# A decoder layer with routed experts: last scatters ahead of a weight split, last destinations ahead of shared rows, and the first four expert tiles waiting for their own expert's splits

## The chip, the cores and the metric

The kernel runs on 1 core of a Trainium2 chip. The metric is device time in microseconds (us), the median of three runs. A core has five engines with a queue each: TensorE (PE), VectorE (DVE), ScalarE (ACT), GpSimd (POOL) and SyncE (SP, which here issues DMA transfers and waits). They meet only in semaphores.

## The reference

The input x is 4 batches of 256 rows of 256 values. One layer adds three sublayers to it, each behind a layer norm without weights:

```
x = x + attn(_layernorm(x))                 # gated memory: sigmoid gates, decaying scan, output product
x = x + xattn(_layernorm(x), ctx)           # softmax over normalised similarities
x = x + ffn(_layernorm(x))

logits = x @ router_w                       # 8 experts
expert_idx = argmax(logits); score = sigmoid(max(logits)); xs = x * score
for e in range(8):
    h = silu(xs @ gate_w[e]) * (xs @ up_w[e])
    out = out + where(expert_idx == e, h @ down_w[e], 0)
shared = silu(x @ shared_gate_w) * (x @ shared_up_w) @ shared_down_w
return out + shared
```

Each of the 1024 rows goes to one expert. All matrices are 256 x 256, but for the router's and the context's.

## The kernel before

**Two stages.** In the first, the four batches pass through steps with names like turn1, similarity, router. Each engine executes its steps in an order written out by hand (PE_ORDER, ACT_ORDER, DVE_ORDER, POOL_ORDER, lines 50 to 76); "name:b" is that step for batch b, and semaphores order the engines among one another. In the second, rows are worked on sorted by expert, in NS = 15 tiles of 128 rows.

**Between them** each batch of 256 rows is routed. TensorE's `rank` counts with matmuls how many rows ahead of each go to the same expert; for the last batch it also counts the rows of each expert. VectorE's `destination` (line 809) makes each row's place from it, and for batch 3 first the counts (`counts_made`). GpSimd's `scatter` (line 456) waits for the destinations and for the metadata (`row_meta`) and writes two tiles of 128 rows with one indirect DMA each to `x_sorted` in HBM. Places without a row get padding: four transfers of SyncE (line 352) and four of ScalarE (line 643, ahead of shared_tanh:3), both behind the counts. VectorE's `slot_table` (line 823) computes for each of the 15 tiles its expert (`te`) and its first row (`tr`); `table_made` says that it is done.

**Shared expert.** For each batch: TensorE's `shared_gu`; ScalarE's `shared_tanh`; VectorE's `shared_hidden`, four products that end in `h_made`; TensorE's `shared_turn`, which waits for them; ScalarE's copy `shared_turned`; TensorE's `shared_down`; and VectorE's `shared_add`, which ends in `base_made`. shared_down:2 also waits for shared_add:1.

**Weights in two parts.** Matrices are multiplied as high and low parts. 21 units of 128 x 512 are loaded (SyncE), rounded (`weight_hi`, ScalarE) and split (`weight_lo`): units 0 to 2 by VectorE, 3 to 20 by GpSimd, line 466, each counting `unit_lo` up by one. Units 3 and 4 are the shared expert's; 5 + 2e and 6 + 2e are expert e's. So unit_lo is 18 when all are there, and 4 + 2e when those of expert e are.

**The expert stage.** SyncE waits for the table, the padding, the scatters and the first four tiles of base_made, and loads four tiles of rows (line 362). TensorE waits for table_made, loads the 15 experts of `te` into registers of its own sequencer (line 1140), waits for all 18 splits (line 1141) and for the down weights, and then runs, per tile: `rows_turn` (transpose), `gate_up`, `hidden_turn`, `down`; ScalarE and VectorE work in between (`rows_hi`, `rows_lo`, `tile_tanh`, `hidden`, `hidden_copy`, `result`). GpSimd adds each tile's result to the output with an indirect DMA (line 480).

Of the kernel before, what the change touches and what calls it, by code (L numbers as in the profile page):

```python
# [24 lines left out]
I32 = mybir.dt.int32  # L25
# [36 lines left out]
    memory:3 turned3_lo:0 residual3:1 sim_stats:2 residual2:3 route:0 sim_scale:2 destination:0  # L62
    turned3_lo:1 residual3:2 sim_stats:3 route:1 shared_hidden:0 sim_scale:3 destination:1
    turned3_lo:2 residual3:3 route:2 shared_hidden:1 destination:2 turned3_lo:3 shared_add:0 route:3
    shared_hidden:2 destination:3 slot_table:3 shared_add:1 shared_hidden:3 shared_add:2
    shared_add:3
""".split()

# [2 lines left out]
    centre:0 sim_rstd:0 weight_lo:7 sim_eps:1 centre:1 weight_lo:8 weight_lo:9 sim_rstd:1 centre:2  # L71
    weight_lo:10 weight_lo:11 weight_lo:12 sim_eps:2 rstd3:0 sim_rstd:2 weight_lo:13 row_meta:0
    sim_eps:3 scatter:0 sim_rstd:3 centre:3 rstd3:1 weight_lo:14 row_meta:1 scatter:1 rstd3:2
    row_meta:2 scatter:2 rstd3:3 row_meta:3 weight_lo:15 scatter:3 weight_lo:16 weight_lo:17
    weight_lo:18 weight_lo:19 weight_lo:20
""".split()

# [7 lines left out]
def decoder_kernel(nc, x, ctx_in, Wv, Wg, bg, Wq, bq, Wo, W_k, b_k, gamma, beta,  # L85
# [3 lines left out]
    E = router_w.shape[1]  # L89
# [16 lines left out]
    ROUNDS = (NS - 3 - PEEL) // TILE_RING  # L106
    RING = 6
    PROJ = 3

    x_sorted = nc.dram_tensor("x_sorted", (E * REGION + P, W), F32, kind="Internal").ap()  # L110
    out_rows = out.rearrange("b s d -> (b s) d")

    with ExitStack() as ctx:
        def sb(name, shape, dt=F32):
            return ctx.enter_context(nc.sbuf_tensor(name, shape, dt))
# [4 lines left out]
        def sem(name):  # L120
            return ctx.enter_context(nc.semaphore(name))
# [11 lines left out]
        xT3_lo = sb("xT3_lo", [P, 2, KT, S], F32R)  # L133
        gqv_hi = sb("gqv_hi", [P, PROJ, KT, D], F32R)
        gqv_lo = sb("gqv_lo", [P, PROJ, KT, D], F32R)
        wo = sb("wo", [P, KT, D])
# [64 lines left out]
        preceding = sb("preceding", [1, NS])  # L201
        tr_f = sb("tr_f", [1, NS])
        te = sb("te", [1, NS], I32)
        tr = sb("tr", [1, NS], I32)
        cnt = sb("cnt", [1, E], I32)
        tid = sb("tid", [P, NS], U32)
# [19 lines left out]
        def ps_row(n):  # L226
            nonlocal spare
            spare += n
            return bT[0:1, spare - n:spare]

        ntile, tile_s, te_f, offset = ps_row(E), ps_row(NS), ps_row(NS), ps_row(NS)
# [7 lines left out]
        unit_hi, proj_lo, unit_lo = sem("unit_hi"), sem("proj_lo"), sem("unit_lo")  # L239
# [32 lines left out]
        def rows(w):  # L272
            return w.rearrange("(k p) n -> p k n", p=P)

        units = [(rows(w), gqv_hi[:, i], gqv_lo[:, i]) for i, w in enumerate((Wg, Wq, Wv))]
# [4 lines left out]
        SHARED_LO = 2  # L280
# [10 lines left out]
        def pad_regions(queue, engine, first, last):  # L291
            _, count = nc.values_load_multi_w_load_instructions(
                cnt[0:1, first:last], engines=[engine], min_val=0, max_val=N,
                skip_runtime_bounds_check_because="a count of tokens is at most all of them")
            for e in range(first, last):
                queue.dma_start(x_sorted[bass.ds(count[e - first] + e * REGION, P), :], pad[:, :]).then_inc(padded, 16)
# [5 lines left out]
        def _(sp):  # L302
# [3 lines left out]
            def load_unit(n):  # L306
                if n >= RING:
                    old = n - RING
                    sp.wait_ge(unit_hi, old + 1)
                    if old < PROJ:  # L310
                        sp.wait_ge(proj_lo, old + 1)
                    else:
                        sp.wait_ge(unit_lo, old - PROJ + 1)
                sp.dma_start(stage[:, n % RING], units[n][0]).then_inc(stage_in[n % RING], 16)

            def load(name, dst, src, scattered_words=False):
                sp.dma_start(dst, src, allow_slow_non_contiguous=scattered_words).then_inc(small_in[name], 16)
# [18 lines left out]
            sp.dma_start(x_sorted[E * REGION:E * REGION + P, :], pad[:, :]).then_inc(padded, 16)  # L336
            for n in range(PROJ, len(units)):
                load_unit(n)
                if n == PROJ + 1:
                    load("shd", shd[:, :, :], rows(sh_down_w))  # L340
# [14 lines left out]
            def first_rows(s, n):  # L355
                _, values = nc.values_load_multi_w_load_instructions(
                    tr[0:1, bass.ds(s, n)], engines=[mybir.EngineType.SP], min_val=0, max_val=E * REGION,
                    skip_runtime_bounds_check_because="slot_table's rows start a tile of a region or the padding behind them")
                return values
# [131 lines left out]
        def _(act):  # L491
# [37 lines left out]
            def turned_wk(_):  # L529
                act.wait_ge(wk_t, 1)  # L530
                a.copy(wkT[:, :], bM[0:C, 0:C]).then_inc(wkT_made, 1)
# [158 lines left out]
        def _(dve):  # L690
            v = nc.vector
# [131 lines left out]
            def slot_table(_):  # L823

                step = [0]
                dve.wait_ge(sm["rank_done"], B)

                def link(ins):
                    step[0] += 1
                    ins.then_inc(table_step, 1)  # L830
                    dve.wait_ge(table_step, step[0])

                link(v.tensor_tensor(cmp_k[:, :, :], io_k[0:1, :, :], ps_count[0:1, :].unsqueeze(2).to_broadcast([1, E, NT]), ALU.is_lt))
                link(v.tensor_reduce(ntile, cmp_k[:, :, :], AX.X, ALU.add))
                link(v.tensor_tensor_scan(incl[:, :], one_e[:, :], ntile, 0.0, ALU.mult, ALU.add))
                link(v.tensor_scalar(tile_s, io_s[:, :], incl[:, E - 1:E], None, ALU.min))

                link(v.tensor_tensor(cmp_s[:, :, :], tile_s.unsqueeze(2).to_broadcast([1, NS, E]),
                                     incl[:, :].unsqueeze(1).to_broadcast([1, NS, E]), ALU.is_ge))
                link(v.tensor_reduce(te_f, cmp_s[:, :, :], AX.X, ALU.add))  # L840
                link(v.tensor_tensor(cmp_s[:, :, :], cmp_s[:, :, :], ntile.unsqueeze(1).to_broadcast([1, NS, E]), ALU.mult))
                link(v.tensor_reduce(preceding[:, :], cmp_s[:, :, :], AX.X, ALU.add))
                link(v.tensor_tensor(offset, tile_s, preceding[:, :], ALU.subtract))
                link(v.tensor_scalar(tr_f[:, :], offset, float(P), None, ALU.mult))
                v.tensor_scalar(te[:, :], te_f, E - 1.0, None, ALU.min)
                v.scalar_tensor_tensor(tr[:, :], te_f, float(REGION), tr_f[:, :], ALU.mult, ALU.add).then_inc(table_made, 1)

            def shared_hidden(b):
# [16 lines left out]
            def split_router():  # L865
# [6 lines left out]
                     "memory": memory, "residual2": residual2, "sim_stats": sim_stats,  # L872
                     "centre_kv": centre_kv, "sim_scale": sim_scale, "residual3": residual3,
                     "turned3_lo": turned3_lo, "route": route, "destination": destination, "slot_table": slot_table,
                     "shared_hidden": shared_hidden, "shared_add": shared_add}
            for name, n in steps_of(DVE_ORDER):
# [24 lines left out]
            with dve.Fori(0, ROUNDS) as i:  # L901
                for j in range(TILE_RING):
                    s = i * TILE_RING + (PEEL + j)
# [11 lines left out]
        def _(pe):  # L915
            T = nc.tensor

            def product(out_ap, pairs):

                terms = [(a, c) for a, _, c, _ in pairs] + [(b, c) for _, b, c, _ in pairs] + [(a, d) for a, _, _, d in pairs]  # L920
                for i, (l, r) in enumerate(terms):
                    last = T.matmul(out_ap, l, r, start=(i == 0), stop=(i == len(terms) - 1))  # L922
                return last
# [186 lines left out]
            def experts(first, n):  # L1110
                _, values = nc.values_load_multi_w_load_instructions(
                    te[0:1, bass.ds(first, n)], engines=[mybir.EngineType.PE], min_val=0, max_val=E - 1,
                    skip_runtime_bounds_check_because="slot_table counts experts up from 0 and clamps to E - 1")
                return values

            def gate_up(s, r, e, reused):
                pe.wait_ge(xg_lo_made, s + 1)
                if reused:
                    pe.wait_ge(rh_made, s - 1)
                product(psGU[r][:, :], [(xgT_hi[:, r, k, :], xgT_lo[:, r, k, :], gu_hi[:, e, k, :], gu_lo[:, e, k, :])  # L1120
                                        for k in range(KT)]).then_inc(gu_done, 1)
# [15 lines left out]
                last.then_inc(down_done, 1)  # L1137

            pe.wait_ge(table_made, 1)
            e = experts(0, NS)  # L1140
            pe.wait_ge(unit_lo, len(units) - PROJ)
            pe.wait_ge(small_in["dn"], 16 * E)
            rows_turn(0, 0, 0, 1, False)
            rows_turn(1, 1, 1, 1, False)
            pe.wait_ge(sm["h_made"], B * TB)
            gate_up(0, 0, e[0], False)
            rows_turn(2, 0, 2, 1, True)
            gate_up(1, 1, e[1], False)
            pe.wait_ge(sm["base_made"], B * TB)
            for s in range(NS + 1):  # L1150
# [36 lines left out]
```

## Time and profile before

| what | us |
|---|---|
| median of 3 runs | 138.51 |
| lowest, highest | 138.19, 139.47 |
| the profiled execution | 139.09 |
| its span, first to last instruction | 137.2 |
| TensorE matmuls busy in it | 116.0 |
| VectorE, ScalarE, GpSimd busy | 82.8, 75.1, 75.3 |

The profile is of one execution. Its times are counted from the first instruction. "Idle before <- releaser" in a timeline is how long the engine stood still and what ended that. The names SPq, ACTq, POOLq and PEldq are the sequencers' own instructions (semaphores, registers, issues of DMAs), which do not count as busy time. The runs' time lies somewhat above the span, since it also holds what is ahead of the first instruction and behind the last.

### The profile page before, as it was taken

The numbers are of one execution on the slowest core, as the hardware profiler recorded it, in microseconds if no ns is written. First come the engines' busy times: TensorE is split into PE (matmuls) and PEld (weight loads), VectorE is DVE, ScalarE is ACT, GpSimd is POOL, SyncE is SP. The second block draws the span as 40 slices with busy tenths as digits, with TensorE's granted clock in tenths as the row PEclk, the third lists the DMA queues.
The fourth block names the chain that finished last, engine by engine and source line by source line (L and its number), as shares of the span: only waits on it lengthen the run. The fifth ranks groups of instructions, "written<-read, shape, count | busy, mean of one in ns | idle before, by whom it ended". The sixth has DMA issues, their size and how long they took to land. (4 is left out here: it accounts for less than half of the span.)

```text
span 137.2 us, 2564 instructions
## 1 busy us (share of the span) xinstructions
PE 116.0 (85%) x663; PEld 94.3 (69%) x663; DVE 82.8 (60%) x290; ACT 75.1 (55%) x193; POOL 75.3 (55%) x118
## 2 busy tenths in 40 slices
PE   0099999999999888988997997499999999999600
PEld 0059889869779574857887865378888888888300
DVE  2673099928979998739785872556454546454000
ACT  3335787695666859149573362144556465655500
POOL 5207070573856793891838799300665466456680
PEclk9999999999999999879999999999999999999975
DMA  4997992065252552104102291963426451351200
GB/s 126 249 264 207 358 302 76 0 202 185 76 160 76 193 190 76 70 16 153 62 22 81 98 313 40 301 213 81 78 56 118 72 88 42 36 63 20 30 1 0
DMA packets 18924, 16.44 MB, mean 120 GB/s; under 512 B 4320, under 2 KB 18656, under 8 KB 18912
## 3 DMA queue, kind: packets, MB, share of 16 engines
q1 hardware_dynamic: 15792, 13.56, 32.1%
q0 software_dynamic: 2544, 2.17, 9.6%
q10 hardware_dynamic: 576, 0.56, 1.2%
q8 instruction: 6, 0.10, 0.3%
q14 instruction: 6, 0.05, 0.1%
HBM read 11.82 MB, written 5.38 MB: 125 GB/s over the span
## 5 line engine op out<-in xcount | busy, mean ns | idle before, releaser
L480 POOL DMA_INDIRECT out_dram<-tq,tid x15 | 23.3, 1556 | 23.4 <-ACT tq L670 12.3
L466 POOL TENSOR_TENSOR gu_lo<-stage,gu_hi 128x512 fp32r<-128x512 f32 x16 | 20.3, 1286 | 2.1 <-ACT gu_hi L527 2.0
L461 POOL DMA_INDIRECT x_sorted<-xs,dest x8 | 8.6, 1074 | 5.3 <-DVE dest L821 3.1
L527 ACT CAST gu_hi<-stage 128x512 fp32r<-128x512 f32 x16 | 9.4, 618 | 0.0
L1136 PE MATMUL bV<-dn,xT 128*128 x32 | 8.3, 383 | 0.8 <-ACT xT L664 0.8
L1086 PE MATMUL bV<-shd,xn 128*128 128x256 f32 x32 | 7.9, 389 | 0.8 <-ACT xn L628 0.7
L928 PE MATMUL bT<-ident,xn 128*128 128x128 f32 x16 | 2.9, 311 | 6.6 <-DVE xn L716 6.6
L658 ACT ACTIVATE tg<-bG,meta 128x256 f32<-128x256 f32 x8 | 3.8, 474 | 7.8 <-PE bG L922 7.8
L884 DVE SCALAR_TENSOR_TENSOR tg<-tg,bG 128x256 f32<-128x256 f32 x8 | 3.4, 422 | 7.6 <-ACT tg L658 7.6
L1003 PE MATMUL bO<-wo,tq 128*128 128x256 f32 x32 | 7.9, 389 | 0.0
L703 DVE BATCH_NORM_STATS2 bn<-res 128x6 f32<-128x256 f32 x16 | 6.0, 415 | 2.5 <-DMA res<-in_x_dram 2.4
L1136 PE MATMUL bO<-dn,xT 128*128 x28 | 7.3, 383 | 0.0
L1086 PEld LDWEIGHTS bV<-shd,xn 128*128 128x128 f32 x32 | 5.8, 190 | 2.1 <-issue 1.4
L1003 PEld LDWEIGHTS bO<-wo,tq 128*128 128x128 f32 x32 | 5.8, 189 | 1.7 <-issue 1.0
L928 PEld LDWEIGHTS bT<-ident,xn 128*128 128x128 f32 x16 | 2.1, 160 | 6.6 <-issue 6.6
L670 ACT ACTIVATE tq<-bV,meta 128x256 f32<-128x256 f32 x8 | 4.5, 565 | 3.7 <-PE bV L1136 3.7
L922 PE MATMUL bG<-gu_hi,xT_hi 128*128 x16 | 5.8, 443 | 0.9 <-DVE xT_lo L890 0.9
L1136 PEld LDWEIGHTS bV<-dn,xT 128*128 128x128 f32 x32 | 5.4, 190 | 1.4 <-issue 1.0
L658 ACT ACTIVATE tg<-bQ,meta 128x256 f32<-128x256 f32 x7 | 3.3, 474 | 5.6 <-PE bQ L922 5.6
L726 DVE TENSOR_TENSOR xT_lo<-bT,xT_hi 128x512 fp32r<-128x512 f32 x4 | 2.8, 690 | 5.5 <-ACT xT_hi L563 5.5
L890 DVE TENSOR_TENSOR xT_lo<-bT,xT_hi 128x256 fp32r<-128x256 f32 x8 | 3.4, 424 | 4.4 <-ACT xT_hi L651 4.4
L421 POOL TENSOR_TENSOR rstd<-vareps,expo 128x2 f32<-128x2 f32 x8 | 5.7, 711 | 0.4
(204 smaller groups left out, 359.5 us busy)
## 6 DMA issues: line engine op xcount, KB each, us to landing
stage<-in_L_ffn_gate_w_dram SPq DMA_DIRECT2D x8, 256.0 KB, 3.4
stage<-in_L_ffn_up_w_dram SPq DMA_DIRECT2D x8, 256.0 KB, 3.1
dn<-in_L_ffn_down_w_dram SPq DMA_DIRECT2D x8, 256.0 KB, 3.4
xs<-x_sorted SPq DMA_DIRECT2D x15, 136.0 KB, 2.2
res<-in_x_dram SPq DMA_DIRECT2D x4, 256.0 KB, 3.8
out_dram<-res SPq DMA_DIRECT2D x4, 256.0 KB, 3.2
x_sorted<-pad SPq DMA_DIRECT2D x5, 136.0 KB, 1.8
x_sorted<-pad ACTq DMA_DIRECT2D x4, 136.0 KB, 2.5
```

The source lines that it names most:

```text
L421: g.tensor_tensor(rstd[:, kind, b, :], vareps[:, kind, b, :], expo[:, :], ALU.pow).then_inc(rstd_made[kind], 1)
L461: g.indirect_dma_start(x_sorted, bass.IndirectOffsetOnAxis(dest[:, t:t + 1], 0), xs[:, t, :], None, bounds_check=E * REGION - 1, oob_is_er ...
L466: g.tensor_tensor(units[n][2], stage[:, n % RING], f32(units[n][1]), ALU.subtract).then_inc(unit_lo, 1)
L480: g.indirect_dma_start(out_rows, bass.IndirectOffsetOnAxis(tid[:, s:s + 1], 0), ry[:, s % TILE_RING, :], None, bounds_check=N - 1, oob_is_ ...
L527: a.copy(units[n][1], stage[:, n % RING]).then_inc(unit_hi, 1)
L658: a.activation(rh[:, r, :], psGU[r][:, 0:D], ACT.Tanh, scale=meta[:, s, 0:1]).then_inc(rth_made, 1)
L703: v.bn_stats(bn[:, kind, b, i, :], tile(i)).then_inc(bn_raw[kind], 1)
L922: last = T.matmul(out_ap, l, r, start=(i == 0), stop=(i == len(terms) - 1))
L928: last = T.transpose(ps[:, k, i * P:(i + 1) * P], rows_of[:, i, k * P:(k + 1) * P], ident[:, :])
L1003: last = T.matmul(psO[:, i, :], tq[:, b % 2, m, i * P:(i + 1) * P], wo[:, m, :], start=(m == 0), stop=(m == KT - 1))
L1086: last = T.matmul(psV[:, i, :], hs[:, b % 2, k, i * P:(i + 1) * P], shd[:, k, :], start=(k == 0), stop=(k == KT - 1))
L1136: last = T.matmul(psY[r][:, 0, :], hT[:, r, k, :], dn[:, e, k, :], start=(k == 0), stop=(k == KT - 1))
```

## The change

Three edits. (1) In VectorE's order destination:3 stands ahead of shared_hidden:2 instead of behind it. (2) In GpSimd's order scatter:3 stands ahead of weight_lo:15. (3) TensorE no longer waits for all 18 splits ahead of its first tile. slot_table makes one array more, `units_ahead`, two times the expert of each of the first four tiles; TensorE loads its four values with one instruction each, ahead of the 15 experts, and gate_up of tiles 0 to 3 waits for 4 more splits than that value. gate_up of tile 4 waits for all 18.

```diff
-    shared_hidden:2 destination:3 slot_table:3 shared_add:1 shared_hidden:3 shared_add:2
+    destination:3 shared_hidden:2 slot_table:3 shared_add:1 shared_hidden:3 shared_add:2
...
-    row_meta:2 scatter:2 rstd3:3 row_meta:3 weight_lo:15 scatter:3 weight_lo:16 weight_lo:17
+    row_meta:2 scatter:2 rstd3:3 row_meta:3 scatter:3 weight_lo:15 weight_lo:16 weight_lo:17
...
+    UNITS = 2
+    EARLY = 4
...
+        units_ahead = sb("units_ahead", [1, EARLY], I32)
...
                 v.tensor_scalar(te[:, :], te_f, E - 1.0, None, ALU.min)
+                v.tensor_scalar(units_ahead[:, :], te_f[:, 0:EARLY], E - 1.0, float(UNITS), ALU.min, ALU.mult)
                 v.scalar_tensor_tensor(tr[:, :], te_f, float(REGION), tr_f[:, :], ALU.mult, ALU.add).then_inc(table_made, 1)
...
             def gate_up(s, r, e, reused):
+                if s < EARLY:
+                    pe.wait_ge(unit_lo, ahead[s] + (SHARED_LO + UNITS))
+                elif s == EARLY:
+                    pe.wait_ge(unit_lo, len(units) - PROJ)
                 pe.wait_ge(xg_lo_made, s + 1)
...
             pe.wait_ge(table_made, 1)
+            ahead = [pe.value_load(units_ahead[0:1, s:s + 1], min_val=0, max_val=UNITS * (E - 1)) for s in range(EARLY)]
             e = experts(0, NS)
-            pe.wait_ge(unit_lo, len(units) - PROJ)
             pe.wait_ge(small_in["dn"], 16 * E)
```

## Rows read from the trace of the kernel before

**Rows 1.** The first line of the page.

```profile
span 137.2 us, 2564 instructions
```

**Rows 2.** The chain of waits around the stage's start: start us, us, what.

```profile
80.57 6.24 POOL gu_lo L466 x5
...
86.85 0.45 PE bT L1107 x2
...
87.73 0.44 DVE xT_lo L890
88.17 0.23 issue
88.40 1.66 PE bG L922 x6
```

**Rows 3.** Busy time in windows: us, PE, PEld, DVE, ACT, POOL, PEclk, DMA share, GB/s.

```profile
95.00:110.00 15.00, 15.00 (x79) 12.38 (x78) 7.61 (x29) 8.57 (x23) 8.16 (x6) 1.00 0.45 83
```

**Rows 4.** Timeline of TensorE, 74 to 84 us: start, us, engine, line, operation, tiles.

```profile
74.80 0.34 PE L1051 MATMUL bT<-onehot,ones 128*128 128x8 bf16 x8
...
76.81 0.60 PE L1075 MATMUL bO<-ident,hrow 128*128 128x128 f32 x4
...
80.30 1.97 PE L1086 MATMUL bV<-shd,xn 128*128 128x256 f32 x8
82.45 0.66 PE L1075 MATMUL bO<-ident,hrow 128*128 128x128 f32 x4 [0.18 <-DVE hrow L855]
83.83 1.97 PE L1086 MATMUL bV<-shd,xn 128*128 128x256 f32 x8 [0.72 <-ACT xn L628]
```

**Rows 5.** Timeline of VectorE, 74 to 87 us.

```profile
74.26 0.41 DVE L853 SCALAR_TENSOR_TENSOR hrow<-hrow,bG 128x256 f32<-128x256 f32 x1
...
75.49 0.42 DVE L855 SCALAR_TENSOR_TENSOR hrow<-hrow,bQ 128x256 f32<-128x256 f32 x1
75.83 0.15 DVE L814 CAST cnt<-bT 1x8 int32<-1x8 f32 x1
...
76.59 0.20 DVE L833 TENSOR_TENSOR cmp_k<-io_k,bT 1x64 f32<-1x64 f32 x1
...
79.22 0.15 DVE L846 SCALAR_TENSOR_TENSOR tr<-bT,tr_f 1x15 int32<-1x15 f32 x1
79.30 0.85 DVE L862 SCALAR_TENSOR_TENSOR res<-bV,half_r,xs 128x256 f32<-128x256 f32 x2
...
81.97 0.42 DVE L855 SCALAR_TENSOR_TENSOR hrow<-hrow,bQ 128x256 f32<-128x256 f32 x1
...
85.83 0.88 DVE L862 SCALAR_TENSOR_TENSOR res<-bV,half_r,xs 128x256 f32<-128x256 f32 x2 [2.65 <-PE bV L1086]
```

**Rows 6.** Timeline of ScalarE, 78 to 81 us: its pad transfers, then shared_tanh:3.

```profile
78.20 1.91 ACTq L296 DMA_DIRECT2D x_sorted<-pad  x4
80.23 0.47 ACT L621 ACTIVATE hrow<-bG,rstd 128x256 f32<-128x256 f32 x1 [2.20 <-PE bQ L922]
```

**Rows 7.** Timelines of GpSimd and SyncE, 71 to 85 us.

```profile
71.99 1.07 POOL L461 DMA_INDIRECT x_sorted<-xs,dest  x1 [0.86 <-issue]
...
76.61 0.20 POOL L454 TENSOR_TENSOR xs<-xs 128x2 f32<-128x2 f32 x1
...
78.22 1.07 POOL L461 DMA_INDIRECT x_sorted<-xs,dest  x1 [0.17 <-issue]
...
84.20 1.95 SPq L362 DMA_DIRECT2D xs<-x_sorted  x4
```

**Rows 8.** Sequencer instructions by line: count: ns min/median/max, first and last start.

```profile
L1111 PEldq TENSOR_LOAD <-te x1: 1759/1759/1759, 83.9 to 83.9; - x1
...
L356 SPq TENSOR_LOAD <-tr x4: 302/686/867, 79.4 to 105.0; - x4
...
L1083 PEldq EVENT_SEMAPHORE  x1: 550/550/550, 83.2 to 83.2; - x1
...
L1103 PEldq EVENT_SEMAPHORE  x1: 51/51/51, 86.4 to 86.4; - x1
```

## The prediction

> **What bounds the kernel now.** The page's first line gives the span: 137.2 us [rows 1]. That execution took 139.09 us, 1.89 us more than its span; the three timed runs have a median of 138.51 us. I sum against 137.2 and carry the difference over to 138.51.
>
> I read the chain of waits next, because it says which wait ends last at each point [rows 2]. GpSimd's five last weight splits run from 80.57 to 86.81; TensorE's first transpose of sorted rows (rows_turn(0)) follows at 86.85. Then come ScalarE's copy, VectorE's split at 87.73 and TensorE's gate_up(0) at 88.40. Behind that the windows view shows TensorE busy for 15.00 of 15.00 us [rows 3], and the expert stage is a fixed train of 15 tiles. So whatever moves gate_up(0) moves the end by the same amount, and nothing behind it can give time back. The question is what releases 86.85 and 88.40 once the splits do not.
>
> The timelines of TensorE, VectorE and ScalarE just ahead of it, and the rows of the sequencers' own instructions, answer this. In every one the reader should look for who is second latest.
>
> **Part 1: destination:3 ahead of shared_hidden:2 (VectorE).** Before, TensorE's counts (rank:3) end at 74.80 + 0.34 = 75.14 [rows 4], while VectorE is in the four hidden products of shared_hidden:2, from 74.26; the last ends at 75.49 + 0.42 = 75.91, and destination:3 runs from 75.83 until slot_table starts at 76.59 [rows 5]. In the new order VectorE waits for the counts, runs destination:3 (76.59 - 75.83 = 0.76) from 75.18 to 75.94, and shared_hidden:2 takes its 75.91 - 74.26 = 1.65 behind that: its last product is there at 77.59 instead of 75.91, 1.68 later. Destinations and counts are there 0.65 earlier.
>
> Who waits for the products? TensorE's shared_turn:2. It began at 76.81, so 0.90 of slack covers the first part of the delay [rows 4]. From an idle start a turn began 0.06 behind its release (82.45 against 81.97 + 0.42 = 82.39 [rows 4, 5]), so it now starts at about 77.65: 0.84 later. With the turn 0.84 to 0.90 later, so are ScalarE's copy of it and, behind that copy on ScalarE, the four pad transfers (78.20) and shared_tanh:3 (80.23) [rows 6]. I take 0.90, since a turn from an idle start also finishes a little later: its 0.66 from 82.45 is longer than the 0.60 of the row at 76.81. slot_table starts at 77.51 and has one small operation more, at most the 0.15 of its neighbour [rows 5]; shared_add:1 behind it moves from 79.30 to 80.3 or 80.4, and shared_down:2, which waits for it, from 80.30 to about 81.3. It lies beside shared_tanh:3 and shared_hidden:3, so the 0.1 beyond 0.90 is covered. shared_hidden:3 ends at 83.29, shared_turn:3 starts at 83.35, and shared_down:3 at 83.83 + 0.90 = 84.73. Alone, this delay would vanish: TensorE stood idle from 83.83 + 1.97 = 85.80 to 86.85 [rows 2, 4].
>
> **Part 2: scatter:3 ahead of weight_lo:15 (GpSimd).** The rows' metadata is ready at 76.61 + 0.20 = 76.81, with the destinations already there (about 76.0). The scatter before stood 0.86 in its issue (71.99), so I put the new one at 77.67 instead of 78.22: 0.55 earlier; the bounds are 0 and 78.22 - 76.81 = 1.41 [rows 7]. SyncE's row loads start at 84.20 behind the scatters. They come at about 83.65, and rows are in SBUF at about 85.85 instead of 86.4, the time at which TensorE's sequencer passed the wait for them (L1103) [rows 7, 8]. ScalarE's pads, 0.90 later, also have to be in. They were by 84.20, so at the worst the loads come at 85.1 and the rows at 87.3, still ahead of the sum below. SyncE's pads follow the counts, 0.65 earlier. weight_lo:15 now lies behind the scatters, and the six splits at 6.24 / 5 = 1.25 each end near 86.81 + 1.25 - 0.55 = 87.5.
>
> **Part 3: own expert's splits.** The wait for all 18 splits goes to gate_up(4), which has four such products of 1.66 us ahead of it alone, so it lies past 88.4 + 4 x 1.66 = 95.0 [rows 2]: 87.5 costs nothing there. Tiles are sorted by expert; the first four need 4 + 2e splits, so even e = 4 (one expert without rows) needs 12, and weight_lo:15, which now ends near 81, is the 13th. None of them waits.
>
> In exchange four value_load instructions stand ahead of the load of all 15 experts, on TensorE's own sequencer. That load takes 1.76 us from 83.9 to 85.66 [rows 8], and starts there because the sequencer stood in shared_down:3's wait (L1083) for 0.55 us, until 83.75, though the table was ready at 79.37 [rows 5, 8]. Before, it was hidden twice, under shared_down:3 and under the wait for the splits. The new kernel moves its start to 83.9 + 0.90 = 84.8 and takes the second cover away. One register alone isn't in the trace. Four together took 0.302 to 0.867 us with a middle of 0.686, fifteen 1.759 (0.117 each) [rows 8]. Bounds for one: 0.302 / 4 = 0.075, and, if a short load is all fixed cost, 0.686. I take 0.2, above the share of 0.117 because a fixed part recurs: 0.8 for four, bounds 0.3 and 2.7. With 0.1 for the semaphore instructions behind them (one is 0.051), rows_turn(0) starts at 84.8 + 0.8 + 1.76 + 0.1 = 87.46, 0.61 later than 86.85.
>
> The Trainium skill, "Runtime: NRT & Kernel Launch", section "Instruction fetch mechanics", puts register loads from HBM at about 200 ns per register even in bulk; these come from SBUF. By it 15 registers would be 3.0 us, and here they took 1.76, so the measurement decides; four would be 0.8. The sum with 3.0 in it would be 1.24 us later.
>
> gate_up(0) to gate_up(3) also gain a register addition and a semaphore instruction. From an idle TensorE the first lay 0.23 behind its data [rows 2]; I add 0.1 once (bounds 0 and 0.3, since the others lie mostly under matmuls already queued).
>
> **Sum:** 0.61 + 0.1 = +0.7: span 137.9, that execution 139.8, the median 138.51 + 0.7 = 139.2 us.
>
> **Rivals.** *A, the loads are dear:* the same place, but each single load costs as much as a load of four. The change is 83.9 + 0.90 + 4x + 1.76 + 0.1 + 0.1 - 86.85 = 4x - 0.09; it passes 1% (1.39 us, about what can be told from no change) from x = 0.37 on. At 0.5 it is +1.9, 140.4 us. For it: two of the rows for four are near 0.69 and 0.87. Against it: 0.302 for four, and 0.117 per register in the long one.
>
> *B, the loads are hidden:* they run under shared_down:3 (1.97 us long), as the long one did for most of its time. The Trainium skill, "Advanced Engine Details and Errata", section "Sequencer and Instruction Queues", says that engine instructions wait in a queue while the sequencer executes control instructions. The trace agrees: the load started 0.07 behind the first of those matmuls. But shared_add:3, 85.83 to 86.71 before [rows 5], moves by 0.90 to 86.73 to 87.61, and the split of the first rows (87.73) stands behind it on VectorE, so it can start at 87.5 at the earliest. Even here the gain is at most 0.2 us: 138.3 us, not slower.
>
> *C, the gain arrives:* VectorE's new order doesn't delay TensorE, because what holds ScalarE's copy or tanh is something else. Then the loads start at 83.9, and rows_turn(0) at 83.9 + 0.8 + 1.76 + 0.1 = 86.56: -0.3 + 0.1 = -0.2, 138.3 us. Against it: the 77.59 of part 1 follows from durations alone. A gain of 1% would need gate_up(0) at 87.0; no case gives it.
>
> **How the numbers follow.** Forecast (+0.3 to +1.2) 0.58, A 0.17, B 0.15, C 0.07, others 0.03. The median comes out as 139.2 us. The range goes from 138.2 (B and C less 0.1) to 140.1, which takes in the lower edge of A. Faster by over 1%: 0.03. Slower by over 1% is the part of A beyond x = 0.37: 0.16. Within 1%: 0.81.
>
> **What would show it.** In the trace after: shared_turn:2 near 77.65, shared_tanh:3 near 81.1; shared_down:3 near 84.7; four short register loads and the long one on TensorE's sequencer from 84.8 to about 87.4; rows_turn(0) right behind them, with GpSimd's last split ending near 87.5, later than it; row loads near 83.65. The forecast is wrong if rows_turn(0) starts before 87 or behind 88, if a gate_up of the first four waits for splits, or if row loads or pads come behind 85.

## The result

The changed kernel takes 145.45 us in the median of 4 runs (145.0 to 146.88), against 138.43 for the kernel before: a ratio of 1.0504, with an interval of 1.0451 to 1.0556. It was forecast at 139.2. Its profiled execution took 145.17 us, with a span of 143.2. That is 6.0 more than the 137.2 of [rows 1], and the 6.0 are accounted for here. The medians lie 7.0 apart, because the profiled execution before (139.09) lay 0.66 above its median and this one 0.28 below. Ratios leave out executions more than 1.5% above their kernel's fastest, and the profiled ones of e2_orders_alone, e7_two_loads and i1_wait_moved_scatters are such.

The page of the changed kernel, its span and TensorE's granted clock in 40 slices of 3.6 us:

```profile
span 143.2 us, 2582 instructions
...
PEclk9999999999999999599999999658999999999985
```

The second group of low digits, slices 26 to 28 (90 to 100 us), is at the start of the expert stage. TensorE's timeline there, changed kernel; it answers [rows 2] and [rows 4]:

```profile
77.48 0.66 PE L1079 MATMUL bO<-ident,hrow 128*128 128x128 f32 x4 [0.68 <-DVE hrow L859]
...
84.68 1.97 PE L1090 MATMUL bV<-shd,xn 128*128 128x256 f32 x8 [0.72 <-ACT xn L631]
90.38 0.41 PE L1111 MATMUL bT<-ident,xs 128*128 128x128 f32 x2 [3.73 <-issue]
...
91.91 1.22 PE L926 MATMUL bG<-gu_hi,xT_hi 128*128 x2 [0.90 <-DVE xT_lo L894]
...
94.91 1.20 PE L926 MATMUL bQ<-gu_hi,xT_hi 128*128 x2
...
97.61 0.46 PE L1136 MATMUL bU<-ident,tg 128*128 128x128 f32 x2
```

shared_down:3 starts at 84.68, but rows_turn(0) only at 90.38, against 86.85 before: 3.73 us of idle time that the profile puts down to no engine ("issue"). And gate_up(0), one row of it shown at 91.91, is followed by hidden_turn(0) only at 97.61, 5.70 us later, where before it was 91.63 - 88.40 = 3.23. The row of hidden_turn(0) and the window of the first products in the kernel before:

```profile
91.63 0.41 PE L1128 MATMUL bU<-ident,tg 128*128 128x128 f32 x2
...
88.40:91.60 3.20, 3.20 (x14) 2.35 (x14) 1.30 (x6) 0.74 (x2) 0.00 (x0) 1.00 0.83 273
```

The sequencer's own instructions say what the idle time was (columns as in [rows 8]):

```profile
L1148 PEldq TENSOR_LOAD <-units_ahead x4: 327/452/782, 84.7 to 87.0; - x4
L1148 PEldq FUSED_REGOPS  x4: 146/151/165, 85.3 to 87.8; - x4
L1148 PEldq SEQ_ASSERT  x4: 18/18/28, 85.5 to 88.0; - x4
...
L1115 PEldq TENSOR_LOAD <-te x1: 2014/2014/2014, 88.1 to 88.1; - x1
```

Each value_load is three instructions: the load (497, 327, 406 and 782 ns, a mean of 0.50 us), register operations for the comparison with the bounds, and an assertion. Four of them take 88.1 - 84.7 = 3.4 us, 0.85 each, so 0.35 of each is the check with the gaps around it. And the load of the 15 experts stands behind them. Windows of the changed kernel (us, PE, PEld, DVE, ACT, POOL, PEclk, DMA share, GB/s) say why the first products are slow:

```profile
90.30:91.90 1.60, 0.63 (x4) 0.42 (x5) 0.67 (x4) 0.65 (x2) 0.00 (x0) 0.70 0.00 0
91.90:94.60 2.70, 2.69 (x6) 2.04 (x7) 0.34 (x3) 0.00 (x0) 0.00 (x0) 0.50 0.39 100
94.60:97.60 3.00, 3.00 (x9) 2.30 (x8) 1.31 (x5) 0.80 (x2) 0.00 (x0) 0.50 0.01 3
97.60:98.05 0.45, 0.45 (x5) 0.43 (x4) 0.00 (x0) 0.20 (x1) 0.00 (x0) 0.81 0.32 44
98.05:103.40 5.35, 5.35 (x30) 4.43 (x29) 3.14 (x12) 3.11 (x9) 1.15 (x1) 1.00 0.17 48
```

The granted clock is 0.50, so 1.2 GHz instead of 2.4, through gate_up(0) and gate_up(1), and full again from gate_up(2) on. The whole loss of the trace is 90.38 - 86.85 = 3.53 for the start, and 5.70 - 3.23 = 2.47 for the products at the lower clock: 6.0 us.

### The profile page after: what moved, and what is told of

It reads as the page before. It is cut to its first block, busy times and chain, and to the rows that moved or that the text cites. A ratio compares the mean times of both kernels' runs of the same rounds, so it can differ in the third digit from the quotient of the medians.

```text
span 143.2 us, 2582 instructions
## 1 busy us (share of the span) xinstructions
PE 118.7 (83%) x663; PEld 96.3 (67%) x663; DVE 82.8 (58%) x291; ACT 75.1 (52%) x193; POOL 75.4 (53%) x118
## 4 chain that ended last, share of the span: by engine, by line
PE 69%; DVE 11%; issue 8%; DMA 3%; ACT 2%; ACTq 2%; POOL 2%; SPq 1%; POOLq 0%; DVEq 0%
PE bG L926 17%; PE bQ L926 16%; PE bV L1144 4%; PE bV L926 4%; PE bO L1007 4%; PE bO L1144 4%; DMA ez<-in_ctx_dram 3%; PE bM L926 3%; PE bV L1090 3%; PE bT L1111 2%; POOL out_dram L483 2%; DVE hrow L859 1%; PE bS L1025 1%; PE bU L1015 1%; PE bO L1079 1%
## 5 line engine op out<-in xcount | busy, mean ns | idle before, releaser
L926 PE MATMUL bG<-gu_hi,xT_hi 128*128 x16 | 6.3, 477 | 0.9 <-DVE xT_lo L894 0.9
L1111 PE MATMUL bT<-ident,xs 128*128 128x128 f32 x16 | 3.3, 293 | 3.7 <-issue 3.7
L888 DVE SCALAR_TENSOR_TENSOR tg<-tg,bQ 128x256 f32<-128x256 f32 x7 | 2.9, 421 | 5.9 <-ACT tg L661 5.9
```

Of the source, the lines that this page charges most:

```text
L888: v.scalar_tensor_tensor(rh[:, r, :], rh[:, r, :], 1.0, psGU[r][:, 0:D], ALU.add, ALU.mult).then_inc(rt_made, 1)
L1111: last = T.transpose(psX[r][:, k, 0:P], xg[:, q, k * P:(k + 1) * P], ident[:, :])
```

## The experiments

The early part of the kernel shifts by up to 2.7 us from one execution to the next. So the traces are compared from the first operation of route:3 on VectorE ("route" below), which no edit touches. "Idle" is TensorE's just ahead of rows_turn(0); "first products" is from gate_up(0) to hidden_turn(0).

| kernel | route | rows_turn(0) behind it | gate_up(0) behind it | idle | first products |
|---|---|---|---|---|---|
| before | 73.34 | 13.51 | 15.06 | 1.06 | 3.23 |
| changed | 73.17 | 17.21 | 18.74 | 3.73 | 5.70 |
| e1_loads_alone | 72.78 | 15.60 | 17.13 | 3.14 | 4.50 |
| e2_orders_alone | 74.98 | 14.22 | 15.77 | 0.76 | 3.22 |
| e10_pool_order_alone | 73.22 | 14.16 | 15.71 | 1.63 | 3.22 |
| e4_unchecked | 72.31 | 14.03 | 15.55 | 0.55 | 3.21 |
| e3_no_loads | 73.34 | 13.72 | 15.24 | 0.24 | 3.22 |
| e6_filled | 73.47 | 17.34 | 18.87 | 0.22 | 3.21 |
| e8_singles_unchecked | 73.11 | 16.36 | 18.04 | 2.88 | 5.71 |
| e7_two_loads | 74.90 | 16.57 | 18.09 | 3.10 | 5.71 |
| e11_stores_later | 72.71 | 14.81 | 16.34 | 1.33 | 4.69 |
| i1_wait_moved_scatters | 74.78 | 12.62 | 14.34 | none | 3.22 |
| i3_experts_in_two | 72.51 | 12.49 | 14.38 | none | 3.20 |
| i4_split_on_vector | 73.78 | 12.49 | 14.79 | none | 3.22 |

**The loads alone.** The kernel before with the four loads added, and nothing that uses them:

```diff
+                v.tensor_scalar(units_ahead[:, :], te_f[:, 0:EARLY], E - 1.0, float(UNITS), ALU.min, ALU.mult)
...
             pe.wait_ge(table_made, 1)
+            ahead = [pe.value_load(units_ahead[0:1, s:s + 1], min_val=0, max_val=UNITS * (E - 1)) for s in range(EARLY)]
             e = experts(0, NS)
```

> The kernel before with one thing added: units_ahead is computed and TensorE's sequencer loads its four values with four value_load instructions ahead of the 15 experts; nothing uses them, and both orders and the wait for all 18 splits are those of before. Theory L (the four loads, each with its own bounds check, take 3.4 us of the sequencer, as 84.7 to 88.1 in the changed kernel, and with the orders untouched start near 83.9): experts loaded by 83.9 + 3.4 + 1.9 = 89.2, rows_turn(0) near 89.4 instead of 86.85, so +2.5 us, and up to 2.3 more if TensorE, idle from 85.8, drops its clock for the first two gate_up: 141.0 to 143.3 us. Rival O (the new orders or the waits against registers cost the time): within 0.9 us of before.

Two of the four runs took 141.86 and 142.56 us, the others 146.54 and 146.88, so no ratio is given; the trace is of the one at 141.86, and what the two long ones did isn't known. Its sequencer rows:

```profile
L1144 PEldq TENSOR_LOAD <-units_ahead x4: 301/314/499, 83.3 to 85.5; - x4
L1115 PEldq TENSOR_LOAD <-te x1: 2007/2007/2007, 86.1 to 86.1; - x1
```

The loads take 86.1 - 83.3 = 2.8 us here, rows_turn(0) lies 2.1 us further back than before, and the clock is low for the first of the two products (0.50 from 89.9 to 92.9; 1.3 us more). Nothing else of the change is in this kernel. Rival O, that the orders or the register waits cost the time, falls. But the loads alone cost less than the 3.70 us by which rows_turn(0) lies further back in the changed kernel. There they start 11.5 us behind route instead of 10.5, since VectorE's order delays shared_down:3, and they take 3.4 us instead of 2.8: 1.6 us between them.

**The orders alone.** Both reorderings, no other edit:

```diff
-    shared_hidden:2 destination:3 slot_table:3
+    destination:3 shared_hidden:2 slot_table:3
...
-row_meta:3 weight_lo:15 scatter:3 weight_lo:16
+row_meta:3 scatter:3 weight_lo:15 weight_lo:16
```

> The kernel before with the two new orders alone (destination:3 ahead of shared_hidden:2, scatter:3 ahead of weight_lo:15); the wait for all 18 splits stays ahead of rows_turn(0). Theory L: the splits end at about 87.4 and rows_turn(0) starts right behind, and shared_down:3 lies 0.85 later: +0.5 to +0.8 us, 139.0 to 139.3. Rival O (the orders cost the 7 us): 143 us or more.

139.61 us, a ratio of 1.0076 (1.0047 to 1.0105), or 1.05 us. Its profiled execution reached route 1.6 us later than that of before, so only the positions in the table are read from it. rows_turn(0) is released by GpSimd's last split, 0.71 later than before.

**GpSimd's order alone.** The second of those edits by itself:

> The kernel before with scatter:3 ahead of weight_lo:15 on GpSimd and nothing else. Both orders together cost 1.05 us. Theory (that loss is the one split that now lies behind the scatters, less the 0.55 us by which they come earlier, because rows_turn(0) waits for the last split): +0.7 us, 139.3. Rival (it is VectorE's order, through shared_down:3 and the load of the experts): within 0.2 us of before.

139.49 us, a ratio of 1.0056 (1.0024 to 1.0088), or 0.8 us, and 0.65 us later in the table. Its row of TensorE names the release:

```profile
87.38 0.44 PE L1107 MATMUL bT<-ident,xs 128*128 128x128 f32 x2 [1.63 <-POOL gu_lo L466]
```

So nearly all the cost of the two orders is the split that now lies behind the scatters, as long as rows_turn(0) waits for all of them. VectorE's order adds 0.06 us in the trace: the delay of shared_down:3 disappears under that wait.

**The change without its loads.** The first four gate_up wait for a constant that covers this data's experts; all else is the changed kernel:

```diff
-                    pe.wait_ge(unit_lo, ahead[s] + (SHARED_LO + UNITS))
+                    pe.wait_ge(unit_lo, 12)
...
-            ahead = [pe.value_load(units_ahead[0:1, s:s + 1], min_val=0, max_val=UNITS * (E - 1)) for s in range(EARLY)]
```

> The changed kernel without the four value_load instructions: the first four gate_up wait for the constant 12 splits, which covers this data's experts. All else is that of the changed kernel, the two orders and units_ahead in slot_table too. Theory L (the four loads and what hangs on them are the whole loss): the load of 15 experts ends near 84.8 + 1.8 to 2.3, rows_turn(0) follows near 87.0 to 87.3, no lower clock: within 0.5 us of before, 138.3 to 139.3 us. Rival (something else in the change costs a good part): 141 us or more.

139.22 us, a ratio of 1.0030 (1.0000 to 1.0059). All that the change costs beyond 0.4 us is in the four loads and what hangs on them. rows_turn(0) comes 0.24 us behind shared_down:3, right behind the load of the experts:

```profile
87.06 0.41 PE L1111 MATMUL bT<-ident,xs 128*128 128x128 f32 x2 [0.24 <-issue]
...
L1115 PEldq TENSOR_LOAD <-te x1: 2021/2021/2021, 84.9 to 84.9; - x1
```

gate_up(0) is still 0.18 us later than before in the table. So even with the four loads at no cost the change would not have gained: VectorE's order puts shared_down:3 and the load of the experts later, and that load now sets the start.

The kernel meant as a first separation of loads and checks turned out to be the same experiment. Its loads had no bounds check and its waits were constants; nothing used the values, and its trace shows none of the four loads:

> The changed kernel with the four loads done without a bounds check (four loads of one register, no comparison and no assertion behind them), and the first four gate_up waiting for the constant 12 splits, which covers this data's experts, instead of the loaded values. It separates the loads from their checks. Theory L1 (the check instructions, 0.15 us of register operations, the assertion and the gaps around them, are a good half of the 0.85 us per value): the loads take 4 x 0.4 = 1.6 us instead of 3.4, rows_turn(0) starts near 88.5, TensorE's idle time falls under 2 us and its clock stays up: about 4 us faster than the changed kernel, 141.2. Theory L2 (the loads themselves are nearly all of it): the loads take 2.0 to 2.8 us, 142 to 144.5.

139.09 us, in four runs from 136.99 to 141.09: too wide for a ratio. It says nothing on L1 and L2.

**Loads without checks.** So the next kernel has single loads that are used: the experts themselves, four one by one and eleven together.

```diff
-            e = experts(0, NS)
+            e = [experts(s, 1)[0] for s in range(EARLY)] + list(experts(EARLY, NS - EARLY))
```

> The changed kernel without its four value_load instructions; instead the first four experts are loaded one register at a time without a bounds check, and the other eleven with one load; the first four gate_up wait for the constant 12 splits. Five loads, no checks. Theory L2 (a load of one register costs nearly as much as a load of four, 0.5 us in the middle here): 4 x 0.5 = 2.1 us with the steps between them, then 11 registers in 1.3 to 1.6: experts there near 84.7 + 3.6 = 88.3, rows_turn(0) near 88.4, 1.5 behind before, TensorE idle for 1.8 us and no lower clock: 140 us. Theory L1 (the cost of 0.85 us per value in the changed kernel is mostly its check): the four loads take 0.5 us in all, experts there at 86.7, 138.5 us.

144.07 us, a ratio of 1.0324 (1.0273 to 1.0376). The sequencer's row for the five loads:

```profile
L1115 PEldq TENSOR_LOAD <-te x5: 313/501/2682, 84.6 to 86.6; - x5
```

The window of the last of them, the load of eleven (the last three columns are PEclk, the DMA engines' busy share and GB/s):

```profile
86.60:89.30 2.70, 0.00 (x0) 0.00 (x0) 0.88 (x2) 0.00 (x0) 0.66 (x1) 1.00 0.95 316
```

Four single loads take 86.6 - 84.6 = 2.0 us, 0.5 each, as L2 says. With checks it was 0.85 each, so the check costs 0.35, as in the changed kernel's own rows. But the time is 4 us beyond the 140 of L2, for two reasons that neither had: the load of only eleven registers took 2.68 us, and the clock fell after 2.88 us of idle time.

**The clock.** Sixteen matmuls that nobody reads, four behind each load, in the changed kernel:

```diff
+            ahead = []
+            for s in range(EARLY):
+                ahead.append(pe.value_load(units_ahead[0:1, s:s + 1], min_val=0, max_val=UNITS * (E - 1)))
+                for i in range(4):
+                    T.matmul(bG[:, :], xT3_hi[:, 1, 0, 0:P], shw_hi[:, 0, :], start=True, stop=True)
```

> The changed kernel with four matmuls of 512 columns behind each of the four loads, whose results nobody reads (they go to a bank that gate_up(0) overwrites). The sequencer's loads stay as they are, so rows_turn(0) still starts near 90.4, but TensorE is not idle for 3.7 us. Theory C (the idle time lowers TensorE's clock from 2.4 to 1.2 GHz, and the first two gate_up take 2.7 us each instead of 1.5 for it): granted clock near 1.00 through 91.9 to 98, gate_up(0) in 1.5 us, about 2.3 us faster than the changed kernel, 143.1. Rival (the first gate_up are slow for another reason, such as the register waits or GpSimd's splits): no gain, 145 us or more.

142.92 us, a ratio to the kernel before of 1.035 (1.0267 to 1.0432), 2.5 us under the changed kernel (2.1 by the ratios, whose intervals do not overlap). Its TensorE timeline:

```profile
86.58 4.01 PE L1150 MATMUL bG<-shw_hi,xT_hi 128*128 128x512 f32 x16
90.81 0.41 PE L1111 MATMUL bT<-ident,xs 128*128 128x128 f32 x2 [0.22 <-issue]
```

And the window of its first products:

```profile
92.30:95.60 3.30, 3.26 (x15) 2.45 (x16) 1.42 (x6) 0.74 (x2) 0.00 (x0) 1.00 0.32 84
```

rows_turn(0) is as late as in the changed kernel (17.34 against 17.21), but the clock stays at 1.00 and the first products take 3.21 us. Work added to the idle time made the kernel faster. That the idle time lowered the clock here is shown, and with it the size of this share. The register waits and GpSimd's splits are all in this kernel too, so the rival falls.

**Two loads instead of four.** EARLY = 2 in the changed kernel:

> The changed kernel with EARLY = 2: two value_load instructions instead of four, and only gate_up(0) and gate_up(1) wait for their own expert's splits. Theory L: the loads take 1.7 us instead of 3.4, rows_turn(0) starts near 88.7, and TensorE stands idle for 2.0 us instead of 3.7. If what lowers the clock is the length of that idle time, both effects shrink: 1.7 us from the loads and up to 2.3 from the clock, 141.4 to 143.7 us. Rival (the register waits themselves slow the first gate_up): 144 us or more.

144.09 us, a ratio of 1.0373 (1.0322 to 1.0423): 1.4 us better than with four by the medians and 1.8 by the ratios, where 1.7 to 4.0 was expected. In the table rows_turn(0) comes only 0.64 us sooner, and the first products not at all; the granted clock is 0.50 through both, which the filled kernel ties to the idle time and not to the register waits. The two loads did take only 1.6 us, 86.4 to 88.0. What took their place is the load of the experts:

```profile
L1115 PEldq TENSOR_LOAD <-te x1: 3350/3350/3350, 88.0 to 88.0; - x1
```

And the window of that load:

```profile
88.00:91.40 3.40, 0.37 (x2) 0.00 (x0) 0.88 (x2) 0.00 (x0) 1.03 (x1) 1.00 0.94 322
```

3.35 us for the same 15 registers as in [rows 8], 1.76 there. The window shows the DMA engines 0.94 busy. In the kernel before it was 0.21:

```profile
83.90:85.70 1.80, 1.80 (x8) 1.34 (x8) 0.00 (x0) 0.00 (x0) 1.80 (x3) 1.00 0.21 58
```

The traffic is SyncE's row loads and, behind them, the four stores of base rows.

**Those stores held back.** The same kernel, with the stores behind rows_turn(1):

```diff
+            sp.wait_ge(tx_done, 2)
             for b in range(B):
                 store_base(b)
```

> The changed kernel with two loads instead of four (as in the experiment before), and SyncE's four stores of the base rows held back until rows_turn(1) is done. In that experiment the load of the 15 experts took 3.35 us, from 88.0 on, beside these stores, with the DMA engines 0.94 busy; before it took 1.76 with them at 0.21. Theory D (register loads from SBUF are slowed by DMA traffic): it takes 1.8 us again, rows_turn(0) starts 1.5 us sooner, TensorE is idle for 1.6 us instead of 3.1 and keeps its clock: 141 us against 144. Rival (its duration varies for another reason): 2.5 us or more, 143 to 144 us.

141.49 us, a ratio of 1.0256 (1.0186 to 1.0327). That is 2.6 us less than with the stores in their old place by the medians and 1.6 by the ratios, whose intervals just touch; in the traces it is 1.76 for the start and 1.02 for the first products. The load:

```profile
L1116 PEldq TENSOR_LOAD <-te x1: 1584/1584/1584, 85.8 to 85.8; - x1
```

And its window:

```profile
85.80:87.40 1.60, 0.39 (x2) 0.00 (x0) 0.88 (x2) 0.00 (x0) 1.04 (x1) 1.00 0.00 0
```

With the DMA engines at 0.00 the load takes 1.58 us, the shortest of all. That traffic lengthens it fits, but one pair of traces doesn't prove it, and the busy share doesn't set the time. The same load took 1.76 us at 0.21 (before), 0.27 (e10) and 0.69 (i1), 1.96 at 0.45 (e6), 2.0 at 0.61 (changed), 0.95 (e3) and 0.96 (e1), 2.21 at 0.98 (e2), 2.33 at 0.90 (e4) and 3.35 at 0.94 (e7). What made that one so long is open. Not all went as expected: the idle time was 1.33 us and the clock still fell for part of both products (4.69 us):

```profile
89.05:92.70 3.65, 3.65 (x11) 2.88 (x12) 0.91 (x5) 0.80 (x2) 0.00 (x0) 0.57 0.85 287
```

And yet e10_pool_order_alone was idle for 1.63 us at the same place and kept its clock. So the length of this one gap doesn't decide; what does is open.

**Without any of that.** The wait for all splits needs neither registers nor a place ahead of rows_turn(0). Kernel i1 (i1_wait_moved_scatters): GpSimd's new order, VectorE's old one, and

```diff
-            pe.wait_ge(unit_lo, len(units) - PROJ)
             pe.wait_ge(small_in["dn"], 16 * E)
...
+            pe.wait_ge(unit_lo, len(units) - PROJ)
             gate_up(0, 0, e[0], False)
```

> The kernel before with two edits: scatter:3 ahead of weight_lo:15, and the wait for all 18 splits moved from ahead of rows_turn(0) to ahead of gate_up(0), where all constants stay constants and no register is loaded. VectorE's order is that of before. Theory L: rows are in SBUF near 85.8 and the experts' load ends between 85.7 and 86.2, so rows_turn(0) starts near 86.0 to 86.4, its split of rows stands behind shared_add:3 on VectorE (86.63), and gate_up(0) starts behind the last split, near 87.5, instead of 88.4: 0.8 us faster, 137.7 us. Rival (the load of fifteen experts sets the start, 1.76 to 2.33 us): 0.3 us faster or nothing.

138.53 us, a ratio of 0.9963 (0.9929 to 0.9997). i3 (i3_experts_in_two) in addition loads the experts in two:

```diff
-            e = experts(0, NS)
+            e = list(experts(0, 4))
...
             gate_up(1, 1, e[1], False)
+            e += experts(4, NS - 4)
```

> The same, and the fifteen experts are loaded in two: four ahead of rows_turn(0), the other eleven behind gate_up(1), when TensorE's queue holds that product. Theory L: the load ahead of rows_turn(0) takes 0.3 to 0.7 us instead of about 2 and is hidden under shared_down:3; gate_up(0) near 87.5 as without it, or 0.2 us earlier where the long load was late; the second load, 1.3 to 1.6 us, lies under gate_up(1), which lasts 1.6: 137.6 us. Rival: the second load is longer than its cover and delays hidden_turn(0): 0.3 us slower than with one load.

138.16 us, a ratio of 0.9957 (0.9926 to 0.9987). Both are about 0.4% faster than the kernel before, 0.5 to 0.6 us where 0.8 and 0.9 were expected, and i1's interval all but reaches 1. gate_up(0) comes 0.7 us sooner in both traces. The two loads in i3 took 0.53 and 1.90 us, and both lay under matmuls. Between i1 and i3 there is no measurable difference. In i3, gate_up(0) waits for the last split:

```profile
86.89 0.72 PE L922 MATMUL bG<-gu_hi,xT_hi 128*128 x2 [0.75 <-POOL gu_lo L466]
```

So in i4 (i4_split_on_vector) VectorE, idle for 2.6 us, does that split:

```diff
-    weight_lo:18 weight_lo:19 weight_lo:20            (GpSimd)
+    weight_lo:18 weight_lo:19
-    shared_add:3                                      (VectorE)
+    late_lo:20 shared_add:3
```

> The kernel with scatter:3 ahead of weight_lo:15, the wait for all splits ahead of gate_up(0) and the experts loaded in two, and now the last split (unit 20) done by VectorE between shared_add:2 and shared_add:3, where it is idle for 2.6 us, instead of by GpSimd. gate_up(0) there waited 0.75 us for GpSimd's last split. Theory: the splits end 1.25 us sooner, gate_up(0) follows its rows' own split, 0.5 us sooner: 137.6 us, 0.9 below before. Rival (VectorE's split has two inputs in SBUF, and waits for GpSimd's or holds them up): no gain against the kernel without it.

138.75 us, a ratio of 0.9996 (0.9966 to 1.0026): no gain over the kernel before, and in the table gate_up(0) comes 0.41 us later than in i3 instead of 0.5 sooner. The intervals of the two kernels overlap. VectorE's timeline, with an early split of the same shape and then the late one, and GpSimd's last three splits:

```profile
10.19 0.66 DVE L722 TENSOR_TENSOR gqv_lo<-stage,gqv_hi 128x512 fp32r<-128x512 f32 x1
...
83.61 3.60 DVE L726 TENSOR_TENSOR gu_lo<-stage,gu_hi 128x512 fp32r<-128x512 f32 x1
87.13 0.87 DVE L866 SCALAR_TENSOR_TENSOR res<-bV,half_r,xs 128x256 f32<-128x256 f32 x2
...
82.94 3.71 POOL L466 TENSOR_TENSOR gu_lo<-stage,gu_hi 128x512 fp32r<-128x512 f32 x3
```

VectorE's split lasts 3.60 us where the early one lasted 0.66. It ends 0.56 us behind GpSimd's, at 87.21 against 86.65, and shared_add:3 and with it the rows' split stand behind it. GpSimd's three took 3.71 us, 1.24 each, no more than elsewhere. So the rival's first half was right, that VectorE waits; nothing was held up on GpSimd.

## Why the prediction was wrong

**The position of everything ahead of the loads was right.** Against route, which lies 0.17 us earlier here, shared_turn:2 was forecast at 77.65 and started at 77.48; shared_down:3 was forecast at 84.73 and started at 84.68. From VectorE, ScalarE, GpSimd and SyncE of the changed kernel, answering [rows 5 to 7]:

```profile
75.00 0.15 DVE L817 CAST cnt<-bT 1x8 int32<-1x8 f32 x1 [0.84 <-PE bT L1055]
...
81.08 0.47 ACT L624 ACTIVATE hrow<-bG,rstd 128x256 f32<-128x256 f32 x1 [2.32 <-PE bQ L926]
...
77.49 1.07 POOL L464 DMA_INDIRECT x_sorted<-xs,dest  x1 [0.86 <-issue]
...
79.85 7.51 POOL L469 TENSOR_TENSOR gu_lo<-stage,gu_hi 128x512 fp32r<-128x512 f32 x6
...
82.90 1.95 SPq L365 DMA_DIRECT2D xs<-x_sorted  x4
```

VectorE waits for the counts for 0.84 us; shared_tanh:3 is at 81.08 (forecast 81.1), the scatter at 77.49 (77.67), the last split ends at 87.36 (87.5). Row loads are at 82.90, 0.75 sooner than forecast: the scatters landed in 2.8 us in the median instead of 4.1. That they now lie ahead of ScalarE's pads fits it (2.9 us in e2, where the pads are later too, 3.8 in e10, where they are not), but wasn't tried alone. It didn't matter, as nobody waits for the rows.

**That the loads on TensorE's sequencer set the start was right.** rows_turn(0) stands right behind them, later than the last split, as part 3 had it. The order of magnitude was not.

**The step that failed is the price of one load**, "I take 0.2", bounds 0.075 and 0.686. It was 0.85, so 3.4 for the four instead of 0.8. Two things are in that. A load of one register costs about 0.5 us, near the price of a load of four: rival A had this condition right, and e8 shows it. And the bounds ended too low, because they were those of loads in the trace of before, all of which skip the bounds check; the changed line gives min_val and max_val without skipping, and that adds register operations and an assertion, 0.35 us per value. The text of the change said so, and I priced a value_load as one instruction. Rival A's own sum with x = 0.85 gives 4x - 0.09 = 3.3 us for gate_up(0); 91.91 - 88.40 = 3.51 was measured, and the rest is mostly the load of the experts, 2.01 us instead of 1.76.

**The step that was missing is the clock.** Neither the forecast nor rival A, which would have left TensorE idle for about 2 us at x = 0.5, asked what the idle time does to TensorE. The sum took every product at its duration of before. That was 2.47 of the 6.0 us, and e6 shows it. The Trainium skill, "TensorE: Matmul & The Clock Gate", section "Why this matters for your kernels", warns of idle gaps between bursts of matmuls. The traces agree for the gaps of 2.88 to 3.73 us, behind which the clock fell each time; of the two short ones, 1.33 us in e11_stores_later lost it in part and 1.63 in e10_pool_order_alone did not.

**Rivals B and C** fall for the changed kernel. B's observation holds all the same: the load of the experts does hide under shared_down:3, and where nothing is put ahead of it (e3) the change costs 0.4 us. The bound from VectorE, that rows' split stands behind shared_add:3, holds in i1 and i3 too, but there GpSimd's last split came later still and released gate_up(0).

**The range** was 138.2 to 140.1. Its upper end was the lower edge of rival A. A at its own upper bound of 0.686 with the clock's 2.5 us on top would have been 143.6. That is still under 145.45, so widening the range by the forecast's own numbers wouldn't have been enough: the bound on a checked load was itself too low.

## What to carry to other kernels

Price a read of one value into a register at half a microsecond of its engine's sequencer, and at 0.35 more if it is checked. Put reads that are needed anyway into one instruction (fifteen took 1.6 to 3.4 us here, four single ones 2.0), and place them where the engine's queue holds work. A wait written with a constant at a later place was cheaper here than an exact one that needs a value: 0.5 us gained against 7.0 lost. If a change can leave TensorE idle for longer than before, add the first products at half clock to the bad case.

## What the runs showed that was not expected

- A checked value_load cost 0.85 us per value (3.4 for four), an unchecked single load 0.5 (2.0 for four). In e1_loads_alone, with the DMA engines 0.24 busy, the checked ones took 0.7 each.
- The same load of 15 registers took from 1.58 us, with idle DMA engines, to 3.35 us, beside stores and row loads (0.94 busy). At about the same share it took 2.0 in two other traces, so the share alone doesn't give the time.
- TensorE's granted clock fell to 0.50 (1.2 GHz) behind 2.9 to 3.7 us without matmuls, for the next 3 to 5.7 us of work, and it did not where 16 unused matmuls filled the time. It also fell in part behind 1.33 us in one trace (0.57 in the 3.65 us from gate_up(0) on), and not behind 1.63 us in another.
- VectorE's split of 128 x 512 with both inputs in SBUF lasted 3.60 us instead of 0.66, until past the end of GpSimd's three splits. The Trainium skill, "SBUF — State Buffer", section "Who interferes with whom", says that a VectorE instruction with two SBUF inputs contends with a GpSimd instruction that reads SBUF, and that the one that comes second blocks. The trace agrees, and goes further: VectorE's instruction ended behind the third in a row, and not behind the one that ran when it started.
